# Layer 0 of a two-layer transformer: its slots reordered, weight loads in quarters, and high parts written by ScalarE

## The reference

```python
x = x + L0_attn(layernorm(x))   # 16 query heads on 8 key/value heads of 128, RMS norm of q and k,
                                # rotation, causal window of 128, softmax, output projection
x = x + L0_ffn(layernorm(x))    # silu(x Wg) * (x Wu), the 2 largest of 4 kept, Wd
x = x + L1_attn(layernorm(x))   # 16 heads, causal mask, softmax, output projection
x = x + L1_ffn(layernorm(x))    # silu(x W1) * (x W3), Walsh-Hadamard transform, W2
```

## Time and profile before

| | |
|---|---|
| median of 3 runs | 689.83 us (689.45 to 691.35) |
| the profiled execution, its own time | 689.38 us |
| its span, first to last instruction | 687.6 us |
| busy PE, PEld, DVE, ACT, POOL | 666.8, 590.8, 550.7, 449.4, 362.4 us |
| mean granted TensorE clock | 0.995 |
| maxima of slot 8 to those of slot 56 of layer 0 | 52.6 to 243.3 us |

### The profile page before, as it was taken

How to read it: one execution, slowest core, us unless ns; L and a number is a source line. 1 busy time by engine, 2 the same in 40 slices (tenths; PEclk the granted TensorE clock), 3 DMA queues, 4 the chain that set the end, 5 groups by cost and what they waited for, 6 DMA issues and landing times.

```text
span 687.6 us, 16092 instructions
## 1 busy us (share of the span) xinstructions
PE 666.8 (97%) x4153; PEld 590.8 (86%) x4153; DVE 550.7 (80%) x1706; ACT 449.4 (65%) x1721; POOL 362.4 (53%) x557
## 2 busy tenths in 40 slices
PE   8899997999999999999999999999999999999998
PEld 4688887988888898788888999999999999978887
DVE  6878876888888888897975989989899989796433
ACT  4888887898898977531327766766666666764222
POOL 5888887899999983200228963425152324027000
PEclk9999999999999999999999999999999999999999
DMA  6165656565656552100025756565656656100000
GB/s 244 36 143 112 138 115 171 114 132 120 146 120 131 134 140 78 48 0 1 1 61 127 142 129 156 118 151 114 153 116 142 133 124 132 38 1 1 1 31 31
DMA packets 239107, 69.18 MB, mean 101 GB/s; under 512 B 184016, under 2 KB 234064, under 8 KB 238928
## 3 DMA queue, kind: packets, MB, share of 16 engines
q1 hardware_dynamic: 215824, 56.53, 37.1%
q10 hardware_dynamic: 23232, 12.06, 5.9%
HBM read 45.29 MB, written 23.27 MB: 100 GB/s over the span
## 4 chain that ended last, share of the span: by engine, by line
PE 63%; DVE 16%; issue 9%; ACT 5%; DMA 3%; SPq 2%; DVEq 1%; POOL 0%; ACTq 0%; POOLq 0%
PE bank L539 13%; PE bank L987 12%; PE bank L422 7%; PE bank L558 7%; DVE scores L788 3%; DMA arrived<-shuffle 3%; ACT probs L604 3%; PE bank L390 3%; DVE rot_b L861 3%; PE bank L1061 3%; PE bank L461 3%; PE bank L1065 3%; PE bank L468 2%; PE bank L383 2%; DVE enc_lo L744 2%
## 5 line engine op out<-in xcount | busy, mean ns | idle before, releaser
L705 ACT ACTIVATE probs<-scores,negmax 128x128 f32<-128x128 f32 (+1 forms) x256 | 116.8, 466 | 5.4 <-DVE negmax L788 4.6
L764 DVE STREAM_TRANSPOSE blocks<-probs 128x384 f32<-128x384 f32 x113 | 65.4, 578 | 51.7 <-ACT probs L604 39.5
L614 ACT CAST enc_hi<-bank 128x256 fp32r<-128x256 f32 x128 | 48.0, 375 | 81.5 <-PE bank L468 73.1
L872 POOL TENSOR_TENSOR a_hi<-raw_a,zero 128x384 fp32r<-128x384 f32 (+1 forms) x60 | 44.6, 744 | 70.9 <-PE bank L558 70.9
L320 POOL TENSOR_TENSOR ln_r<-ln_ve,neg_half 128x1 f32<-128x1 f32 x26 | 17.1, 656 | 117.3 <-DVE ln_ve L294 117.3
L422 PE MATMUL bank<-b_hi,enc_hi 128*128 128x256 f32 x256 | 73.4, 287 | 0.5 <-DVE x L733 0.5
L422 PE MATMUL bank<-b_hi,enc_lo 128*128 128x256 f32 x256 | 72.1, 282 | 0.0
L422 PE MATMUL bank<-b_lo,enc_hi 128*128 128x256 f32 x256 | 72.0, 281 | 0.0
L890 POOL TENSOR_TENSOR rot_a<-rot_a,rot_b 128x384 f32<-128x384 f32 x64 | 65.3, 1021 | 7.7 <-DVE rot_b L861 4.4
L733 DVE SCALAR_TENSOR_TENSOR x<-bank,rinv,x 128x256 f32<-128x256 f32 x144 | 67.4, 468 | 2.3 <-PE bank L422 1.0
L744 DVE TENSOR_TENSOR enc_lo<-bank,enc_hi 128x256 fp32r<-128x256 f32 x128 | 52.0, 406 | 16.8 <-PE bank L390 11.3
(11 more groups left out here) (186 smaller groups left out, 2326.9 us busy)
## 6 DMA issues: line engine op xcount, KB each, us to landing
arrived<-shuffle SPq DMA_DIRECT2D x452, 48.0 KB, 2.2
shuffle<-blocks ACTq DMA_DIRECT2D x57, 192.0 KB, 2.5
shuffle<-blocks SPq DMA_DIRECT2D x56, 192.0 KB, 2.1
raw_a<-in_wa SPq DMA_DIRECT2D x40, 192.0 KB, 3.1
raw_a<-in_wa SPq DMA_DIRECT2D x9, 512.0 KB, 4.1
raw_b<-in_wb SPq DMA_DIRECT2D x16, 256.0 KB, 3.2
hid_last<-in_wax SPq DMA_DIRECT2D x2, 512.0 KB, 5.4
w_a<-in_w2t SPq DMA_DIRECT2D x1, 1024.0 KB, 5.9
```

Source lines behind the costliest of these rows:

```text
L705: nc.scalar.activation(probs[:, c % 4, c0:c1], scores[:, c % 2, c0:c1], ACT.Exp, bias=negmax[:, c % 2, r:r + 1], scale=-1.0, accum_out=row ...
L764: nc.vector.transpose(blocks[:, c % 2, :], probs[:, c % 4, :]).then_inc(s_blocks[L], 1)
```

## The change

In layer 0 alone, for units below 56 (slots below 59):

- PE: values are made for unit c - 4 ahead of output(c - 6) in slot c, where it was unit c - 3 behind it.
- ACT: the copies of the heads(c + 2) come first in the slot, then the scaling, the squares, v, exp; enc_hi(c - 4) is now behind exp, and behind it in odd slots `act_weight_hi` writes the high part of a quarter of the next pair's weight.
- DVE: the wait for the scores comes first, then residual, maxima, low parts of the heads, blocks(c - 1), the two rotation terms, the reciprocal, and enc_lo(c - 4) at the end.
- POOL: writes no high part of a projection weight any more; its low part waits for ACT's high part.
- SP: the projection weight of pairs 2 and up comes in four DMAs of 128 KB at c % 8 = 4, 5, 6, 7; output weights at c % 8 == 1, two slots later than before; the two halves of the late columns at c = 19 and c = 27.

```diff
-A_PARTS = (1, 4)
+A_PARTS = (4, 4)
...
+            if normalized(L, it, c - 4):
+                pe_values(pe, L, it, c - 4)
             pe_output(pe, L, it, c)
...
             pe_turn_probs(pe, L, it, c)
-            pe_values(pe, L, it, c)
+            if not normalized(L, it, c - 3):
+                pe_values(pe, L, it, c - 3)
             pe_turn_heads(pe, L, it, c)
...
-            if c <= TAIL_SLOT or L == 1:
+            if (L == 0 and c in (TAIL_SLOT - 1, TAIL_SLOT)) or L == 1:
                 act_encoded(act, L, it, c - 4)
             if L == 0:
+                act_turned_heads(act, it, c + 2)
                 act_scale(act, it, c - 1)
...
+            if L == 0 and c < TAIL_SLOT - 1:
+                act_encoded(act, 0, it, c - 4)
+            if L == 0:
+                act_weight_hi(act, it, c)
...
             if c < TAIL_SLOT:
+                if L == 0:
+                    dve_scores_wait(dve, L, it, c)
                 dve_residual(dve, L, it, c, 0)
                 dve_rinv(dve, L, it, c)
                 dve_residual(dve, L, it, c, 1)
                 dve_turned_lo(dve, L, it, c - 3)
+                if L == 1:
+                    dve_scores_wait(dve, L, it, c)
+                if L == 1 or c == TAIL_SLOT - 1:
+                    dve_enc_lo(dve, L, it, c)
+                dve_maxima(dve, L, it, c)
+                dve_heads_lo(dve, L, it, c)
                 if L == 0:
                     dve_blocks(dve, 0, it, c - 1)
-                dve_scores_wait(dve, L, it, c)
-                dve_enc_lo(dve, L, it, c)
-                dve_maxima(dve, L, it, c)
-                dve_heads_lo(dve, L, it, c)
...
                 dve_norm(dve, it, c)
+                if c < TAIL_SLOT - 1:
+                    dve_enc_lo(dve, 0, it, c)
...
+        def weight_part(L, it, c):
+            m = c + 5
+            second = L == 1 and it is None and -2 <= c < 2
+            if second or (it is not None or 8 <= m < 64) and m % 2 == 0:
+                return (1, c + 2) if second else (m // 8 + 1, m % 8 // 2)
+            return None
...
+        def act_weight_hi(act, it, c):
+            found = weight_part(0, it, c)
+            if found:
+                pair, part = found
+                slot, cs = pair % 2, slice(part * WA[0] // 4, (part + 1) * WA[0] // 4)
+                if part == 0:
+                    need_weight(act, 0, it, pair)
+                nc.scalar.copy(a_w[slot][0][:, cs], raw_a[:, slot, cs]).then_inc(at[0]["ahi"], 1)
...
+                if L == 0:
+                    need_pairs(pool, s["ahi"], it, done, 4)
+                    nc.gpsimd.tensor_tensor(a_w[slot][1][:, cs], raw_a[:, slot, cs], a_w[slot][0][:, cs].bitcast(F32),
+                                            ALU.subtract).then_inc(s["a"], 1)
...
-                if c % 8 == 4 and c // 8 + 3 < PAIRS + 2:
-                    load_a(0, None, c // 8 + 3, 0)
-                if c % 8 == 7 and c // 8 + 2 < PAIRS:
-                    load_b(0, None, c // 8 + 2)
+                if c % 8 >= 4 and c // 8 + 3 < PAIRS + 2:
+                    load_a(0, None, c // 8 + 3, c % 8 - 4)
+                if c % 8 == 1 and 2 <= c // 8 + 1 < PAIRS:
+                    load_b(0, None, c // 8 + 1)
+                if c in (19, 27):
+                    load_late(0, (c - 19) // 8)
```

More of the change, by code:

```diff
@@ L94, in normalized, with raw_a_loaded @@
     return L == 0 and moved(L, it, m)
+def raw_a_loaded(L, pair):
+    return 16 * A_PARTS[L] * (pair // 2 + 1) - (0 if L else 48)
 def in_parts(L, it, m):
@@ L614, in act_encoded, with act_turned_heads @@
                 nc.scalar.copy(enc[0][:, hh, b * D:(b + 1) * D], bank[O_BANK][:, 0:D]).then_inc(s["ehi"], 1)
+        def act_turned_heads(act, it, m):
+            s = at[0]
+            if live(it, m):
+                t = m % 8
+                need(act, s["tq"], it, m + 1)
+                need(act, s["scores"], it, m - t % 2 - 6)
+                src = bank[TQ_BANK][:, 0:384].rearrange("p (a t) -> p a t", a=3)
+                ts, odd = slice(t // 2 * P, (t // 2 + 1) * P), t % 2
+                if it is None and m < SPLIT_SCORES:
+                    nc.scalar.copy(qk1[:, odd, 0:3, ts], src).then_inc(s["tqev"], 1)
+                else:
+                    nc.scalar.copy(k0_parts[:, 0, t * P:(t + 1) * P], src[:, 2, :])
+                    if odd:
+                        nc.scalar.copy(q_parts[:, 0:2, ts], src[:, 0:2, :]).then_inc(s["tqev"], 1)
+                    else:
+                        nc.scalar.copy(qk1[:, 0, 0:3, ts], src).then_inc(s["tqev"], 1)
         def act_slot(act, L, it, c):
@@ L673, in act_slot @@
                         nc.scalar.copy(v_plain(1, m // 8 % 2, t), src).then_inc(s["vev"], 1)
[L674 to L690, removed]
             if L == 0 and it is None and UNITS - 2 <= c < UNITS:
@@ L874, in split, with need_weight @@
             nc.gpsimd.tensor_tensor(lo, src, hi.bitcast(F32), ALU.subtract).then_inc(s_lo, 1)
+        def weight_part(L, it, c):
[4 more added lines that the diff above has]
+            return None
+        def need_weight(eng, L, it, pair):
+            s, slot = at[L], pair % 2
+            need_pairs(eng, raw_as[L][slot], it, raw_a_loaded(L, pair), 8 * A_PARTS[L])
+            need(eng, s["proj"], it, 8 * (pair - 1))
+            if L == 0 and it is None and pair == 2:
+                eng.wait_ge(s["a"], 4)
+            if L == 1:
+                need(eng, s["vproj"], it, 8 * (pair - 1))
+            if L == 1 and it is None and pair == 1:
+                eng.wait_ge(ff[0]["up"], 16)
+        def act_weight_hi(act, it, c):
[6 more added lines that the diff above has]
+                nc.scalar.copy(a_w[slot][0][:, cs], raw_a[:, slot, cs]).then_inc(at[0]["ahi"], 1)
         def pool_slot(pool, L, it, c):
@@ L895, in pool_slot @@
                                             rms_r[:, t, 2:3].broadcast_to([P, DH]), ALU.mult).then_inc(s["roped"], 1)
[L897 to L900, removed]
+            found = weight_part(L, it, c)
+            if found:
+                pair, part = found
                 w, slot = WA[L] // 4, pair % 2
[L902 to L910, removed]
+                if part == 0 and L == 1:
+                    need_weight(pool, L, it, pair)
                 cs = slice(part * w, (part + 1) * w)
                 done = 4 * (pair - 1) + part + 1
-                split(a_w[slot][0][:, cs], a_w[slot][1][:, cs], raw_a[:, slot, cs], pool, s["ahi"],
-                      lambda: need_pairs(pool, s["ahi"], it, done, 4), s["a"])
+                if L == 0:
+                    need_pairs(pool, s["ahi"], it, done, 4)
+                    nc.gpsimd.tensor_tensor(a_w[slot][1][:, cs], raw_a[:, slot, cs], a_w[slot][0][:, cs].bitcast(F32),
+                                            ALU.subtract).then_inc(s["a"], 1)
+                else:
+                    split(a_w[slot][0][:, cs], a_w[slot][1][:, cs], raw_a[:, slot, cs], pool, s["ahi"],
+                          lambda: need_pairs(pool, s["ahi"], it, done, 4), s["a"])
             m = c - 6
@@ L1603, in load_b, with load_late @@
                 sp.dma_start(raw_b[:, slot, 0:WB], wb[L][n]).then_inc(raw_bs[L][slot], 16)
-            def load_late(L):
+            def load_late(L, *halves):
                 late = (WA_FFN - WA[L]) // 512
-                for h in range(2):
+                for h in halves:
                     sp.dma_start(hid_last[:, late * h:late * (h + 1), :].rearrange("p j t -> p (j t)"),
@@ L1636, in sp_slot0 @@
                     fetch_turned(0, c - 1)
-                if c % 8 == 4 and c // 8 + 3 < PAIRS + 2:
-                    load_a(0, None, c // 8 + 3, 0)
-                if c % 8 == 7 and c // 8 + 2 < PAIRS:
-                    load_b(0, None, c // 8 + 2)
-            load_a(0, None, 1, 0)
+                if c % 8 >= 4 and c // 8 + 3 < PAIRS + 2:
[4 more added lines that the diff above has]
+                    load_late(0, (c - 19) // 8)
+            sp.dma_start(raw_a[:, 1, 0:WA[0]], wa[0][1]).then_inc(raw_as[0][1], 16)
             load_b(0, None, 1)
-            load_a(0, None, 2, 0)
+            for part in range(A_PARTS[0]):
+                load_a(0, None, 2, part)
             for c in range(MOVED[0] + 1):
                 sp_slot0(c)
-                if c == 20:
-                    load_late(0)
             sp.dma_start(w2_a[:, :, :].rearrange("p a d -> p (a d)"), w2t).then_inc(s_w2, 16)
@@ L1659, in _ @@
             sp.wait_ge(ff[0]["down"], 16)
-            load_late(1)
+            load_late(1, 0, 1)
             for part in range(A_PARTS[1]):
```

9 lines of the change are left out of this document (4 added, 5 removed).

## The result

| | before | after |
|---|---|---|
| median of 20 runs | 691.02 us | 692.75 us |
| ratio, 95% interval | | 1.0042 [1.0026, 1.0058] |
| span of the profiled execution | 687.6 us | 689.9 us |
| maxima of slot 8 to those of slot 56 | 190.69 us | 192.80 us |
| mean granted TensorE clock | 0.995 | 0.992 |

I had forecast 686.8 us, range 680 to 691.5. The time lies above the range, by stops that none of my cases had.

A forecast was written before the change was run, and what follows sets the result against it. It took a DVE-ACT loop of 7.69 us per pair of slots as the bound, plus 5.99 us of stalls in slots 8 to 24. -5.99 + 2.4 + 0.65 = -2.9 us led to 686.8 us, range 680 to 691.5.

The forecast's parts named there:

- Heads, scaling, squares and v are in another order, but the same work: ACT's part of the new two-slot loop: reordering adds no time, 152.98 to 155.10, 2.12 us as before.
- I cost it at nothing: DVE's rotation terms come up to 0.58 us later behind the maxima; costed at zero, with 0.39 us a slot to spare.
- Rival (b): POOL waits longer for ACT's high part than counted; at 8.1 us a pair the time is 694.3 us; chance 0.20.
- (c): Arrivals of loads still stall slots 8 to 24: half the loss gives 689.8 us, all of it 692.8; chance 0.10.
- three signs of being wrong: A pair of slots under 7.6 us, a pair over 7.95 us, or `arrived` still appearing as a releaser.
- DMA stalls, -5.99 us: Slots 8 to 24: later value product and split loads give back all 5.99 us lost waiting for arrivals.
- Pace, +2.4 us: Slots 8 to 55: a new loop over POOL, PE and ACT takes 7.79 us a pair against 7.69, +2.4 us.
- four terms: Steps of the new two-slot loop: POOL 3.39, PE 0.60, ACT 3.32, high part to low part 0.48; sum 7.79 us.
- DVE's reordering removes the stall: Work of 0.87 us, maxima and low part alone, now covers DVE's 0.64 us wait ahead of `blocks` in each slot.
- High parts "had to go" from POOL: POOL, busy 107.68 of 119.34 us, would be the next limit; it loses 0.70 us in two slots.
- Head, 0 with 1 us to either side: Slots 0 to 7: first value product's wait goes while the new loop sets in; costed at 0, 1 us either side.
- Tail, +0.65 us: Slot 59: PE makes the values of two units, 55 and 56, adding 0.65 us where PE is the limit.

## Why the prediction was wrong, by its steps

- **The step that failed** is the costing of the reordered programs at nothing but their instructions: "Heads, scaling, squares and v are in another order, but the same work" on ACT, and "I cost it at nothing" for DVE's reordering. The time in the slots was indeed about the same. But 16 instructions more in ScalarE's loop and a VectorE loop that starts three instructions earlier cost 10.4 us in two jumps, and there was no term, bound or rival for that. Rival (b) was a dearer loop over the engines, and the loop came out cheaper than forecast; (c) was stalls that stay, and they went. The sign of the result rests wholly on this: without the stops the change is worth 0.87%. And none of my three signs of being wrong showed: a pair took 7.62, inside my 7.6 to 7.95, and `arrived` was no releaser in slots 8 to 24. They watched the terms that I had, and the failure lay in one that I hadn't.
- **DMA stalls, -5.99 us: right.** None is left in after; the loads alone gave 5.6. Why they went was half right. The loads alone took the long stall, that of slot 17 and half of the other two; the later value product alone took all three short ones, and its slack is no cover for 1 MB of late columns.
- **Pace, +2.4 us: mis-sized.** The loop and its row were right, "POOL a_lo waits for ACT a_hi" in every odd slot with 0.8 us. The terms add up to 7.61 and not 7.79, so 24 x (7.62 - 7.69) = -1.7 us. The 0.07 us that separates gain from loss here is less than what I knew any of the four terms to.
- **DVE's reordering removes the stall: right**, and worth 4.9 us once nothing else is slower.
- **High parts "had to go" from POOL: wrong** at this pace; it cost 4.2 us where it was put.
- **Head, 0 with 1 us to either side**: -1.7 us. Slots 0 to 7 themselves won 2.3 us (29.7 to 27.4), well beyond; 0.5 of it was lost ahead of slot 0, whose maxima started between 22.4 and 24.2 us in kernels with the order of after. **Tail, +0.65 us**: +1.9, of which slots 56 to 63 carry 2.1 (23.7 us against 21.6). TensorE's second set of values isn't all of it: in slot 59 ACT takes enc_hi(55) ahead of the heads, and it waits there:

```profile
255.58 0.37 ACT L621 CAST enc_hi<-bank 128x256 fp32r<-128x256 f32 x1 [1.08 <-PE bank L472]
255.85 0.27 ACT L635 CAST k_parts<-bank 128x128 fp32r<-128x128 f32 x1
```

  The row names a cause; another order there wasn't tried on the chip.
- **The sum** of what the runs showed, from slot 8 to 56: 182.38 - 190.69 = -8.3 us for loads, slack and pace, where I had -3.6, and +10.4 for the two stops: +2.1. With -1.7 and +1.9 at the ends that is the +2.3 us of the spans.

What stays open is why the place decides, though the places narrow it down. VectorE's loop of 293 has jumps of 2.75 us and more from 203, and of at most 0.29 us from 206 (and from 207, where it lay in the kernel with `blocks` first). ScalarE's jumps take 0.21 to 0.23 us where its branch stands at 572 or 573 (and at 557 with the high parts back on GpSimd), and 2.56 to 3.57 us where it stands at 586, 587, 592 or 598; the length doesn't decide by itself, since with 361 they are short from 211 and long from 225. So every placement fits a turn between 203 and 206 in where VectorE's loop starts, and one between 573 and 586 in where ScalarE's branch stands. That is a reading of the table: no run measures such a place by itself. My expectations speak of a boundary and of blocks in which code is held; no run shows either, nor how an engine holds its code.

The other stop of VectorE, 2.4 us behind a jump of 3.02, may be a second fetch. By the records of q14 a packet ends at 115.81 us and the loop's first instruction goes at 117.26; the next but one ends at 118.34 and the second instruction goes at 119.64. At the second jump it is 182.13 and 183.39, then 184.51 and 185.84: each time 1.3 to 1.5 us behind a packet. The scores that the second instruction waits for had been there since 115.55. The records don't say for which engine a packet is, so this too is read from the times, and why VectorE stops after a single instruction was not shown.

## What to carry to other kernels

In this kernel, with rolled loops of 293 to 377 instructions on VectorE and ScalarE, length and place of a loop were a cost of their own: of slots 8 to 56, 6.9 us for VectorE's (192.80 to 185.94) and 3.5 for ScalarE's. An edit can change them, also one that only reorders or sits ahead of the loop. Compare the instruction packets of the DMA queues between two kernels first, and where "issue" of some us stands behind a loop's last line, look at how long the jump takes: an edit should be judged with its loops placed as well as those of its rival, since here a loss of 0.4% was a gain of 0.9% with a fault on top. When work is handed to another engine, ask where in that engine's slot it lands, since one moved instruction was worth 7.3 us (182.38 to 175.07), more than the handing over.

## What the hardware showed that I had not expected

- A jump back of layer 0's loop on VectorE or ScalarE took 0.21 to 0.29 us in some placements and 2.56 to 3.57 us in others. The page's row "q14 instruction" counted 29 to 31 packets where both engines' jumps were short, 40 or 41 where one engine's were long, and 50 or 51 where both were; in the trace of after, these packets have 8192 bytes.
- Three added instructions ahead of a loop of 293 took 6.9 us off slots 8 to 56 (192.80 to 185.94); 14 added ahead of a loop of 361 put 6.4 us on them (190.69 to 197.10), and 26 put 3.9 (194.54), each by one profiled execution.
- In the four kernels where ScalarE alone had long jumps, its next instruction went 1.1 to 1.5 us behind the end of a packet of 8 KB. In both kernels with its loop at 203, VectorE stopped a second time, for 2.3 to 2.4 us, after one instruction.
- On TensorE and GpSimd, layer 0's loops of the same kernels showed no such jump (at most 0.19 us on TensorE, 0.22 and 0.26 on GpSimd); layer 1's loops on VectorE and ScalarE took 0.19 to 0.25 us in every kernel.
